# A four-layer language-model tower on one core: four units in flight with two PSUM banks each, a gate applied before the down projection, and a binary stage with its sign and gates in its input

## The reference

```python
# M0
topk_vals, topk_idx = jax.lax.top_k(gate_logits, K)                # K = 2 of 16
topk_w = jax.nn.softmax(topk_vals, axis=-1)
h = jax.nn.relu(jnp.einsum('bsh,ehf->bsef', x, w1) + b1)
expert_out = jnp.einsum('bsef,efh->bseh', h, w2) + b2
...
moe = jnp.sum(topk_w[..., None] * sel, axis=2)
# M3
gate = bin_gate(sigmoid(einsum('hbi,ei->hbe', xh, proj_w) + proj_b))   # 0 or 1, 8 gates
w = jnp.einsum('hbe,heio->hbio', gate, weight)                     # 64 x 64 weights per token
xb, wb = sign(xh), sign(w)
y = jnp.einsum('hbi,hbio->hbo', xb, wb) * scale
```

## Times and profile before

| | before |
|---|---|
| median of 3 runs | 1112.27 us (1108.61 to 1116.48) |
| span of the profiled execution, first to last instruction | 1084.7 us |
| median less that span | 27.6 us |
| PE, DVE, ACT, POOL busy | 848.1, 540.8, 405.2, 251.5 us |
| mean granted TensorE clock | 0.684 of full speed |

### The profile page before, as it was taken

How to read it: one execution, slowest core, us unless ns; L and a number is a source line. 1 busy time by engine, 2 the same in 40 slices (tenths; PEclk the granted TensorE clock), 3 DMA queues, 4 the chain that set the end, 5 groups by cost and what they waited for, 6 DMA issues and landing times.

```text
span 1084.7 us, 10320 instructions
## 1 busy us (share of the span) xinstructions
PE 848.1 (78%) x3706; PEld 478.3 (44%) x3706; DVE 540.8 (50%) x1074; ACT 405.2 (37%) x655; POOL 251.5 (23%) x193
## 2 busy tenths in 40 slices
PE   0579799955878995498998698993878995274898
PEld 0469676534435221347645585672533223123121
DVE  8652444266466434726465563356575443435333
ACT  2345232222324553233575142242324553130554
POOL 8146412252021201104112402254021001203000
PEclk9979676765596555659799676785568556565555
DMA  7000000000000000000000000000000000000000
GB/s 203 24 10 11 1 1 1 1 1 1 0 1 1 0 0 11 0 1 1 1 1 11 0 1 1 1 1 0 2 0 1 0 1 10 0 1 0 1 0 10
DMA packets 7051, 8.34 MB, mean 8 GB/s; under 512 B 5160, under 2 KB 5672, under 8 KB 6824
## 3 DMA queue, kind: packets, MB, share of 16 engines
q1 hardware_dynamic: 5400, 5.08, 1.8%
q10 hardware_dynamic: 576, 1.55, 0.7%
q0 software_dynamic: 1024, 1.05, 0.4%
HBM read 6.43 MB, written 1.25 MB: 7 GB/s over the span
## 4 chain that ended last, share of the span: by engine, by line
PE 68%; DVE 18%; POOL 5%; ACT 5%; issue 3%; DMA 1%; DVEq 0%; ACTq 0%; POOLq 0%
PE ps L1029 11%; PE ps L1022 11%; PE ps L831 10%; PE ps L744 7%; PE ps L745 5%; POOL inv_std L461 4%; PE ps L736 2%; PE ps L877 2%; PE ps L978 2%; DVE xn L1162 2%; DVE total L1159 2%; PE ps L969 1%; DVE xn L1172 1%; PE ps L754 1%; PE ps L911 1%
## 5 line engine op out<-in xcount | busy, mean ns | idle before, releaser
L704 ACT ACTIVATE hid<-ps 128x512 bf16<-128x512 f32 x256 | 150.1, 598 | 108.3 <-PE ps L1022 106.6
L1486 DVE TENSOR_TENSOR hid<-hid 128x512 bf16<-128x512 bf16 x256 | 112.3, 441 | 144.7 <-ACT hid L704 142.6
L831 PEld LDWEIGHTS ps<-kb,hid 128*128 128x128 f32 x1024 | 155.3, 223 | 28.3 <-issue 14.9
L461 POOL TENSOR_TENSOR inv_std<-var,neg_half 128x8 f32<-128x8 f32 x44 | 73.2, 1668 | 402.6 <-DVE var L1166 402.3
L831 PE MATMUL ps<-kb,hid 128*128 128x64 f32 x1024 | 153.8, 303 | 5.5 <-DVE big_b L1289 3.3
L1029 PE MATMUL ps<-hid,kbin 128*64 128x512 bf16 x256 | 144.8, 577 | 2.2 <-DVE hid L1486 2.2
L1022 PE MATMUL ps<-gTb,w_rows 32*128 32x512 bf16 x256 | 136.4, 543 | 3.4 <-ACT hid L695 1.8
L611 ACT ACTIVATE hid<-ps,kb 128x512 f32<-128x512 f32 x128 | 86.4, 685 | 113.3 <-PE ps L745 112.5
L744 PE MATMUL ps<-xs,up_hi 128*128 128x512 f32 x192 | 114.9, 598 | 17.5 <-ACT hid L611 6.6
L736 PE MATMUL ps<-ka,xn 128*128 128x128 f32 x144 | 34.9, 388 | 108.6 <-DVE xn L1172 108.6
L745 PE MATMUL ps<-xs,up_lo 128*128 128x512 f32 x192 | 94.3, 491 | 0.0
(11 more groups left out here) (262 smaller groups left out, 1140.4 us busy)
## 6 DMA issues: line engine op xcount, KB each, us to landing
hid<-wup SPq DMA_DIRECT2D x2, 782.0 KB, 13.8
out<-h SPq DMA_DIRECT2D x4, 256.0 KB, 2.6
kd<-wd ACTq DMA_DIRECT2D x1, 1007.0 KB, 17.2
kb<-wb SPq DMA_DIRECT2D x1, 885.0 KB, 19.1
bin_raw<-binary SPq DMA_DIRECT2D x1, 576.0 KB, 20.1
w_rows<-w_bounce SPq DMA_DIRECT2D x2, 192.0 KB
ka<-wa SPq DMA_DIRECT2D x1, 320.0 KB, 3.5
krow<-wrow ACTq DMA_DIRECT2D x1, 312.0 KB, 9.2
```

The lines of the kernel that those rows point to most:

```text
L461: G.tensor_tensor(inv_std[g][:, :], var[g][:, :], neg_half[:, :], ALU.pow).then_inc(norm_rstd[g], 1)
L704: act.activation(sg[g][:, i % 4, :], bank[Z_BANK[i % 3]], ACT.Sign).then_inc(m3_s[g], 1)
L831: last = pe.matmul(bank[2 + l][:, to:to + D], hid[g][:, l, e % 4, tile(t)], kb[:, a:a + D], start=True, stop=True)
L1486: V.tensor_tensor(pr[g][:, i % 4, :], sg[g][:, i % 4, :], sx[g][:, l, :], ALU.mult).then_inc(m3_p[g], 1)
```

## The change

Four units are in flight, one in each of four sets of buffers, and each has two PSUM banks: `b0` takes whatever is worked on, `b1` takes what is accumulated. The ring of `hid` buffers has two entries instead of four. The due times are gone; a string for each engine (`TURNS`) says unit by unit whose next piece stands next in the queue.

In M0 a step is: two `up` matmuls into `b0`, ACT's relu into `hid`, a matmul `replicate` that spreads the expert's gate of each token over all 128 hidden features into `b0` (L739, 64 contraction rows, bf16), DVE's multiply of `hid` by it (L1208), and, once per expert, `down` (L707): `w2` stationary, `hid` moving, both lanes side by side, accumulated over the experts in `b1`. POOL's additions are gone, and a turn back to tokens by features is added. The next step's `up` waits for DVE's multiply of the step before.

In M3 the signs of the inputs are spread once for each group of eight input features (`spots3`, L968), DVE multiplies them by the gates (L1398), and a matmul with 128 contraction rows in fp32r (`w3z`, L979) makes input sign times weight for two features and 64 outputs; ACT takes the sign (L658), and `add_up` (L956) adds both lanes side by side into `b1`. DVE's 64 multiplies per unit are gone. The next matmul into `b0` waits for the sign of the one before. The projection to the gates is made in two matmuls instead of one. The split of M3's weights no longer goes through DRAM.

In M1 ACT takes all steps' relus. POOL issues all 32 gathers before the first LayerNorm's root.

```diff
-SLOTS = 2
-BANKS = 4
+BANKS = 2
+RING = 2
...
+def in_order(engine, setup, programs):
+    streams = {"s": setup, **{str(u): program for u, program in enumerate(programs)}}
...
+    for name in TURNS[engine]:
+        next(streams[name], None)
...
-                        for t in tiles:
-                            to = 256 * (e % 2) + D * t
-                            last = pe.matmul(bank[2 + l][:, to:to + D], hid[g][:, l, e % 4, tile(t)],
-                                             kb[:, a:a + D], start=True, stop=True)
+                        for l in lanes:
+                            last = pe.matmul(ps[u][half(l), 1, :], weights, hid[u][:, l, m % RING, :],
+                                             start=False, stop=stop)
+                    def replicate(name, l, m):
+                        pe.matmul(b0, chosen(name, half(l), m), gTb[u][half(l), :],
+                                  start=True, stop=True).then_inc(rep_made[u], 1)
+                    for i in range(LANES * E0):
+                        e, l = divmod(i, LANES)
+                        yield
+                        if i:
+                            pe.wait_ge(hid_gated[u], R_M0 + i - 1)
+                        up("w1_0", e, l).then_inc(z_made[u], 1)
+                        if i == 0:
+                            yield from gates
+                        if i >= LANES and l == 0:
+                            down("w2_0", e - 1, False)
+                        yield
+                        pe.wait_ge(hid_made[u], Z_M0 + i)
+                        replicate("sel0", l, e)
...
+                    def gated(i, m, made, first):
+                        yield
+                        dve.wait_ge(hid_made[u], made + i)
+                        dve.wait_ge(rep_made[u], first + i)
+                        to = hid[u][:, i % LANES, m % RING, :]
+                        V.tensor_tensor(to, b0, to, ALU.mult).then_inc(hid_gated[u], 1)
...
-                        if i >= 3:
-                            pe.wait_ge(m3_s[g], nth(r, LANES * PAIRS, i - 3))
-                        pe.matmul(bank[Z_BANK[i % 3]], w3_rows[rs, P * p:P * (p + 1)], gTb[g][rs, :],
-                                  start=True, stop=True).then_inc(m3_w[g], 1)
-                        pe.matmul(ps[g][half(l), 2, :], cbin("pick3", slice(0, P))[:, a:a + D], pr[g][:, i % 4, :],
-                                  start=(p == 0), stop=(p == PAIRS - 1)).then_inc(m3_sum[g], 1)
+                    def add_up(j, b):
+                        n = LANES * BLOCKS * j + BLOCKS + b
+                        pe.wait_ge(s_made[u], n + 1)
+                        for l in lanes:
+                            last = pe.matmul(ps[u][half(l), 1, :], kbin[:, c:c + D], sg[u][:, BLOCKS * l + b, :],
+                                             start=(j == 0 and b == 0), stop=(j == GROUPS - 1 and b == BLOCKS - 1))
+                        last.then_inc(sum_made[u], 1)
+                            pe.matmul(b0, chosen("spots3", half(l), j), sx[u][half(l), :], start=True, stop=True).then_inc(rep_made[u], 1)
+                                if b == 0:
+                                    pe.wait_ge(u_made[u], LANES * j + l + 1)
+                                else:
+                                    pe.wait_ge(s_made[u], n)
+                                pe.matmul(b0, w3z[:, j, 2 * b:2 * (b + 1), :].rearrange("p i o -> p (i o)"),
+                                          xs[u][:, l, :], start=True, stop=True).then_inc(w_made[u], 1)
...
-                            V.tensor_tensor(pr[g][:, i % 4, :], sg[g][:, i % 4, :], sx[g][:, l, :],
-                                            ALU.mult).then_inc(m3_p[g], 1)
+                            V.tensor_tensor(xs[u][:, l, :], b0, big_a[u][:, l, :], ALU.mult).then_inc(u_made[u], 1)
...
-                    gather(0)
-                    yield 30
-                    gather(1)
+                    for u in units:
+                        if u:
+                            yield
+                        for j in range(SEQS):
+                            pool.indirect_dma_start(
...
```

More of the change, by code:

```diff
@@ L526, in program @@
-                    yield from rstd(AT_M3, LN_M3)
-                in_order(setup(), [program(u) for u in range(UNITS)])
+                        pool.wait_ge(dve_step[u], (DV_SCAN3A, DV_SCAN3B)[l])
+                        G.tensor_tensor(per_tile(big_b[u][:, l, :]), per_tile(scan3[u][:, l, :]),
+                                        sines[:, None, :].broadcast_to([P, TILES, P]), ALU.mult).then_inc(pool_step[u], 1)
+                    yield from rstd(LN_M3)
+                in_order("POOL", setup(), [program(u) for u in units])
@@ L593, in program @@
[L593 to L605 removed]
+                    b0, b1 = ps[u][:, 0, :], ps[u][:, 1, :]
@@ L726, in setup @@
                               start=True, stop=True).then_inc(qk_folded, 1)
                 def program(u):
-                    g, r = u % SLOTS, u // SLOTS
-                    bank = [ps[g][:, i, :] for i in range(BANKS)]
-                    def turn(at, src, ready, value):
-                        yield at + TURN
-                        pe.wait_ge(ready, value)
-                        for t in tiles:
-                            last = pe.transpose(bank[0][:, tile(t)], pair(src[g], t), ident)
-                        last.then_inc(x_turned[g], 1)
@@ L844, in program @@
-                    for t in tiles:
-                        last = pe.matmul(bank[0][:, tile(t)], gT[g][0:ROWS, tile(t)], cb("b2_0", ROWS),
-                                         start=True, stop=True)
-                    last.then_inc(pe_step[g], 1)
-                    yield from turn_norm(AT_A1, LN_A1)
-                    yield AT_A1 + 9
+                    last.then_inc(pe_step[u], 1)
+                    yield from turn_norm(LN_M0)
+                    yield from routes(XS_M0, "route0", E0)
@@ L905, in program @@
-                    for m in range(MT):
-                        yield AT_M1 + 26 + m
-                        for l in lanes:
-                            pe.wait_ge((m1_even, m1_odd)[m % 2][g], nth(r, MT, LANES * (m // 2) + l))
-                        for l in lanes:
-                            a = CD["w2_1"][0] + D * m
-                            last = pe.matmul(ps[g][half(l), 2, :], kd[:, a:a + D], hid[g][:, l, m, :],
-                                             start=False, stop=(m == MT - 1))
@@ new lines, in program @@
+                    for i in range(LANES * MT):
+                        m, l = divmod(i, LANES)
+                        if i:
+                            yield
+                            pe.wait_ge(hid_made[u], Z_M1 + i - 1)
+                        up("w1_1", m, l)
+                        pe.matmul(b0, chosen("sel1", quarter(l), m), gTb[u][quarter(l), :],
+                                  start=False, stop=True).then_inc(z_made[u], 1)
+                        if i >= LANES and l == 0:
+                            down("w2_1", m - 1, False)
@@ L920, in program @@
+                    yield
+                    pe.wait_ge(hid_made[u], Z_M1 + LANES * MT - 1)
+                    down("w2_1", MT - 1, True)
+                    yield from turn_back(AC_F1)
+                    yield from turn_norm(LN_A2)
+                    yield
+                    pe.wait_ge(x_ready[u], XT_A2)
+                    pe.matmul(b1, cd("q2"), xT[u][:, :], start=True, stop=True).then_inc(pe_step[u], 1)
                     for t in tiles:
-                        last = pe.matmul(bank[2][:, tile(t)], xT[g][:, tile(t)], cd("k2"), start=True, stop=True)
@@ L973, in program @@
-                    for m in range(MT):
-                        yield AT_M2 + 34 + m
-                        pe.wait_ge(m2_hg[g], nth(r, LANES * MT, LANES * m + 1))
-                        for l in lanes:
-                            a = CD["w2_2"][0] + D * m
-                            last = pe.matmul(ps[g][half(l), 2, :], kd[:, a:a + D], hid[g][:, l, m, :],
-                                             start=False, stop=(m == MT - 1))
-                    last.then_inc(pe_step[g], 1)
-                    yield from turn_back(AT_M2 + 38, AC_F2)
@@ new lines, in program @@
+                    last.then_inc(pe_step[u], 1)
+                    yield from turn_norm(LN_M2)
+                    yield from routes(XS_M2, "route2", E2)
+                    yield from turn_gates(G_M2, g3)
+                    yield
+                    pe.wait_ge(act_step[u], AC_G2)
+                    pe.matmul(b1, cd("b2_2"), fm2[u][:, :], start=True, stop=False)
+                    for i in range(LANES * MT):
+                        m, l = divmod(i, LANES)
+                        if i:
+                            yield
+                            pe.wait_ge(hid_gated[u], R_M2 + i - 1)
+                        up("w1_2", m, l).then_inc(z_made[u], 1)
+                        if i >= LANES and l == 0:
```

(19 more changed lines are left out.)

1769 lines of the change are left out of this document (830 added, 939 removed), and 28 rows, old and new, of tables (PLACES, TIMES).

## The result

The changed kernel takes 823.14 us (median of 4 runs, 812.77 to 824.32) against 1114.38 us of the kernel before beside it: a ratio of 0.7372 with a 95% interval of 0.7322 to 0.7422. The ratio leaves out one slow run of the kernel before, the one of 1127.9 us. The forecast was 850 us in a range of 740 to 1,000.

The account below looks back on a forecast made before the run. PE's work, then its idle time, bound the kernel: 805 us at the old clock, 883 with 10% idle, 774 at clock 0.78, plus 54 for start and end and 27.6: 855, leaned to 850; range 740 to 1,000.

Parts of the forecast that it names:

- A: Likeliest case: PE filled by four units at a clock between 0.684 and 0.93, 790 to 915 us, chance 0.53.
- What bounds it: Whole kernel: PE's work first, 848.1 of 1084.7 us, its 236.6 us of idle time second, and the clock, mean 0.684.
- The start: Sixteen more gathers ahead of the first root: +17 us, first root at about 47, PE's work from about 50, uncovered.
- M0: M0's work on PE: replicate and half a down pair per step replace L831's records, -18 us, range -40 to +5.
- M3's term: M3's work on PE: 1.75 slots per sign instead of two, -35 us, with -9 put in the range.
- A slot keeps its price: M3 on PE: each matmul slot costs as before, so 1.75 slots per sign save 12.5%, 35 us.
- the 197 us: M3's 256 signs at 1.75 slots of 0.44 us each at half clock, instead of 246 us.
- The clock: Mean clock rises from 0.684 to 0.78, PE's time scaling with it: 883 us become 774.
- The idle time: PE idle 10% after the start, as other units' work covers the hand-overs: 883 us at the old clock.
- The 27.6 us around the span: Added to the forecast span: the timed median of 1112.3 us exceeds the one profiled span by 27.6.
- B: Rival: PE filled but no clock gained, 970 us, or 1,000 with M0's and M3's bad ends, chance 0.24.
- D: Rival: fixed order leaves PE at one unit's pace, M3 sign 1.52 us, 1,123 to 1,171 us in all, chance 0.11.

Follow-up runs that it names:

- Two units in flight: Changed kernel with the pieces of units 0 and 1 first in every engine's queue, then those of units 2 and 3: 1237.6 us, 1.1156 of before.
- no stagger: Changed kernel with all setup first, then one piece of each of the four units in turn on every engine: 962.0 us, 0.8679 of before.
- both row experiments: Changed kernel with w3z cut from 128 to 32 contraction rows: 902.1 to 921.9 us; kernel before with weights3 widened from 32 to 128: 1004.5 us.
- three and then one: Changed kernel with the pieces of units 0, 1 and 2 first in every queue and unit 3 alone after them: 1230.3 us.

## Why the prediction was right, and where its sum was not

The direction, the range and the likeliest case (A: four units fill PE at a higher clock) held. By step:

- **What bounds it** held: PE's idle time and the clock were the gain. PE's busy time multiplied by the mean clock is 848 × 0.684 = 580 us before and 677 × 0.873 = 591 after, so its work did not shrink. "Two units in flight" is 128 us slower than the kernel before, with an order that was not made for it, and "no stagger" shows that up to 139 us hang on the order.
- **The start** held: first root at 47.53 (47 forecast), first PE work at 50.16 (50). That the 17 us lie on the path whole did not: PE's first work came 15 and 16 us earlier, and the time fell by 0 and 4 us.
- **M0** held: −36 us where −18 was taken in a range of −40 to +5; a part of it is the higher clock's, and how much was not measured. The cover of its hand-over was shown.
- **M3's term was mis-sized**, in a way that the clock hid. "A slot keeps its price", so that 1.75 slots in place of 2 save 12.5%, is wrong. At half clock, with 32 rows, the new M3 makes 99 signs in 100 us of filled PE, 1.01 us each, where the old pair took 1.10. In the changed kernel, from 700 to 800, it makes 152 in 98.86 us, 0.65 each, and the old pair at full clock took 0.65 as well. At like clock that is a saving of 8% and of next to none. The reason is the load of `w3z`'s weights. The loads in the run with two units at half clock, and the load ahead of the earlier trace rows before (timelines):

```profile
519.90 0.29 PEld L979 LDWEIGHTS ps<-xs,w3z 128*128 128x128 f32 x1 [0.44 <-ACT hid L658]
520.62 0.10 PEld L968 LDWEIGHTS ps<-fm,kbin 64*128 64x128 bf16 x1 [0.44 <-issue]
```

```profile
360.41 0.13 PEld L1029 LDWEIGHTS ps<-hid,kbin 128*64 128x64 bf16 x1 [0.44 <-issue]
```

  A slot here is a load and 0.44 us behind it: 0.13 + 0.44 = 0.57 from L1029 (360.41) to L1022 (360.98), and 0.29 + 0.44 = 0.73 from `w3z` to `spots3`. The prediction read this 0.44, which is the idle time of the loads, as the time from the start of the previous matmul, which began with its load at 360.41, 0.57 us earlier. So its 0.44 for a slot and the 197 us from it have no row behind them. That the load was not pulled ahead there was read rightly.
- **M3's gain is nearly all the clock's.** Its PE time fell from 281.2 to 198.7 us, by 82. The prediction named the 128 rows as a guess for a higher clock, and both row experiments bear it out, at 79 and 105 us.
- **The clock** was set too low, 0.78 for 0.873, and **the scaling of PE's time with it** too steep. 805 × 0.684 = 551 us at full clock were forecast; 677 × 0.873 = 591 came. A pair falls from 1.10 to 0.65, a factor of 1.7 and not 2. The two errors cancel: the forecast's span was 774 + 54 = 828 us, and 821 came. That it came so near is luck.
- **The idle time** after the start is 97 of 771 us, 12.5%, for 10%.
- **The 27.6 us around the span failed.** Each run of both kernels whose span is listed lasts 1.8 us longer than its span (823.14 and 821.3; before, 1109.87 and 1108.1 at a clock of 0.661). The profiled execution of before, 1084.7 at 0.684, was a faster one than the timed runs: a later run of the same kernel took 1088.47 with a span of 1086.7 at 0.681. The difference went with the clock, and was added as a constant. With 1.8 in its place the sum is 774 + 54 + 1.8 = 830.
- **DVE** 484 us for 508, **ACT** 398 for 415, **POOL** 177 for "well under 200": right, and none reached PE's sum, as said.
- **The rivals.** B's ground was real, not its size: in two units' M3 the clock is 0.50, and waits stand at turns of a bank (0.26 us at 523.21). That the waits are its cause was not shown. The Trainium skill ("TensorE: Matmul & The Clock Gate", "A second HAM failure mode: psum-queue depth-cycling") tells of short pauses between groups of matmuls with which the clock goes back and forth. The trace agrees in part: the pauses are there, but the clock stays at 0.50 through that window, and with four units and the same two banks each it is 0.95. B's bad end was added up too low: 49 us more of PE at 10% idle is 54, so 1,025 and not 1,000, and the range did not take in all of B. D is what fewer units in flight do: 1,238 us with two, 1,230 with three and then one, with 1.83 us per sign alone for its 1.52.

## What to carry to other kernels

Before pricing instructions by their count, look at which clock a stage ran at and what stood in the array then: here an edit that changed only the number of contraction rows moved the time by 105 us. A step that hands over through three engines cost no more here than its own time on PE, with four units in turn; with two, in the order tried, PE stands at it. Price a slot with the load of its weights. Take the constant around a span from runs that list both, and not from a profile set against other runs' median.

## What the runs showed of the hardware

PE filled and the clock low went together: M3 at 100% busy had 0.50 where `weights3` or `w3z` has 32 contraction rows (before, 350 to 400; the changed kernel cut to 32, 700 to 800). With 128 rows it had 1.00 in the old M3, 64 of the rows zeros (350 to 360, 100% busy), and 0.95 in the new one (700 to 800, 99% busy).

At full clock in the changed kernel, `w3z` starts 0.23 us after another `w3z` at the least, and `up`'s second matmul 0.23 after its first; these are fp32r on both sides. From `w3z` to `add_up`, from `add_up` to `w3z` and from `spots3` to either it is 0.31 to 0.32, and between the two bf16 matmuls of the old M3 at full clock 0.31 to 0.34 (smallest intervals between starts, 23 to 166 of each). The 0.23 is not the rule: it holds for 30 of the 103 intervals between two `w3z`, whose median is 0.34. Four `w3z` in a row in the changed kernel's timeline, what follows, and the loads of the four:

```profile
742.09 1.20 PE L979 MATMUL ps<-xs,w3z 128*128 128x512 f32 x4
743.21 0.41 PE L956 MATMUL ps<-hid,kbin 128*64 128x512 bf16 x2
742.08 0.76 PEld L979 LDWEIGHTS ps<-xs,w3z 128*128 128x128 f32 x4 [0.23 <-issue]
```

The four loads run without a gap from 742.08 to 742.84, beside the matmuls, where at half clock in M3 0.44 us lay between two loads.

So the rule that the prediction weighed, weights that load while the matmul ahead runs (the Trainium skill, "TensorE: Matmul & The Clock Gate", step "① LDWEIGHTS — get the stationary operand into the array"), agrees with the trace in these intervals between fp32r matmuls. It does not at the hand-overs of M3 in which a bf16 matmul takes part, and in the old M3 that was every slot.
